# Prologue of a fused attention layer: GpSimd presets split in two, cond's silu and turn later, the embedding in another bank and reader step, five warm-up matmuls left out

## The reference: what is computed

```python
xn = layer_norm(x, norm_w, norm_b)                      # x: 8 x 512 x 256
q, k = xn @ q_w + q_b, xn @ k_w + k_b                   # 16 heads of 16
att = einsum('bnhl,bmhl->bnmh', q, k) + (1 - mask) * -1e6
att = softmax(att, axis=2)
v = (xn @ v_w + v_b) * src_mask
y = einsum('bnmh,bmhl->bnhl', att, v)
e = silu(emb) @ emb_w + emb_b                           # emb (cond): 8 x 512
scale, shift = split(e, 2)
h = layer_norm(y, sb_norm_w, sb_norm_b) * (1 + scale) + shift
out = x + silu(h) @ out_w + out_b
```

## Time and profile before

| | |
|---|---|
| time, median of 3 | 563.47 us |
| the profiled execution: its own time / its span | 564.25 / 562.5 us |
| TensorE matmul busy (PE) | 524.0 us, 93% |
| VectorE busy (DVE) | 416.9 us, 74% |
| ScalarE busy (ACT) | 371.4 us, 66% |
| GpSimd busy (POOL) | 194.2 us, 35% |
| mean granted TensorE clock | 0.997 |

### The profile page before, as it was taken

The page is one execution under the profiler, slowest core; times in us unless marked ns, Lnnn a source line. Parts: engine busy times, 40 slices in busy tenths (PEclk is TensorE's granted clock), DMA queues, the critical chain, the costliest instruction groups (busy, mean ns, idle before and its releaser), DMA issues.

```text
span 562.5 us, 10004 instructions
## 1 busy us (share of the span) xinstructions
PE 524.0 (93%) x2845; PEld 194.7 (35%) x2848; DVE 416.9 (74%) x661; ACT 371.4 (66%) x674; POOL 194.2 (35%) x237
## 2 busy tenths in 40 slices
PE   7888999999999999999999999999999999988886
PEld 3452223233343334333343233433342333422243
DVE  7588667787788778787787777877687867878425
ACT  2205776677757877577766877577766877667851
POOL 7244112443342512334333422425233422224003
PEclk9899999999999999999999999999999999999999
DMA  5632332433324332433424333333325323241021
GB/s 135 215 116 86 105 121 79 120 97 108 113 61 152 105 121 78 130 114 98 113 74 150 98 117 88 105 124 103 111 82 155 93 79 95 88 132 47 1 76 38
DMA packets 55050, 57.95 MB, mean 103 GB/s; under 512 B 12376, under 2 KB 42200, under 8 KB 55024
## 3 DMA queue, kind: packets, MB, share of 16 engines
q1 hardware_dynamic: 54480, 56.84, 34.0%
q10 hardware_dynamic: 544, 0.79, 0.5%
HBM read 36.35 MB, written 21.00 MB: 102 GB/s over the span
## 4 chain that ended last, share of the span: by engine, by line
PE 74%; DVE 11%; issue 7%; ACT 5%; DMA 1%; POOL 0%; ACTq 0%; POOLq 0%; DVEq 0%; SPq 0%
PE pv_ps L492 22%; PE st_ps L476 16%; PE mx_ps L450 11%; PE job_ps L533 9%; DVE negmax L776 8%; ACT probs L608 5%; PE job_ps L540 5%; PE job_ps L563 4%; PE mx_ps L460 1%; PE pv_ps L397 1%; PE job_ps L551 1%; DMA x_in<-in_x 1%; PE mx_ps L533 1%; PE mx_ps L540 0%; PE job_ps L424 0%
## 5 line engine op out<-in xcount | busy, mean ns | idle before, releaser
L776 DVE TENSOR_REDUCE negmax<-mx_ps 128x2 f32<-128x1024 f32 x256 | 301.4, 1220 | 106.9 <-PE mx_ps L450 106.3
L608 ACT ACTIVATE probs<-st_ps 128x512 f32<-128x512 f32 x512 | 277.9, 597 | 101.2 <-PE st_ps L476 98.2
L476 PE MATMUL st_ps<-q_rows,k_rows 115*128 115x512 bf16 x512 | 166.5, 384 | 14.1 <-ACT probs L608 6.0
L492 PE MATMUL pv_ps<-probs,v_rows 128*32 128x512 f32 x1024 | 136.4, 605 | 0.5 <-ACT probs L608 0.5
L1024 POOL TENSOR_TENSOR qk_rest<-qk_full,qk_parts 128x512 f32<-128x512 f32 x31 | 35.9, 1157 | 202.5 <-ACT qk_parts L620 202.5
L476 PEld LDWEIGHTS st_ps<-q_rows,k_rows 115*128 115x128 bf16 x512 | 39.5, 97 | 127.6 <-ACT probs L608 84.4
L450 PE MATMUL mx_ps<-k_rows,q_rows 51*128 51x512 bf16 x512 | 80.0, 381 | 2.0 <-DVE negmax L776 1.1
L533 PE MATMUL job_ps<-x_norm_t,w_qk 128*128 128x512 f32 x116 | 54.7, 593 | 0.6 <-DVE mod_half L763 0.6
L450 PEld LDWEIGHTS mx_ps<-k_rows,q_rows 51*128 51x128 bf16 x512 | 16.5, 94 | 109.4 <-issue 65.5
L1033 POOL TENSOR_TENSOR qk_parts<-qk_rest,qk_parts 128x512 bf16<-128x512 f32 x31 | 35.9, 1158 | 46.8 <-DVE qk_parts L851 38.9
L631 ACT ACTIVATE qk_full<-job_ps,qkb_col 128x512 f32<-128x512 f32 x29 | 19.9, 687 | 25.9 <-PE job_ps L533 25.9
(11 more groups left out here) (112 smaller groups left out, 400.1 us busy)
## 6 DMA issues: line engine op xcount, KB each, us to landing
qk_dram<-qk_parts SPq DMA_DIRECT2D x128, 128.0 KB
q_rows<-qk_dram SPq DMA_DIRECT2D x124, 96.0 KB
k_rows<-qk_dram SPq DMA_DIRECT2D x124, 96.0 KB
x_in<-in_x SPq DMA_DIRECT2D x16, 256.0 KB, 2.9
x_res<-in_x SPq DMA_DIRECT2D x8, 512.0 KB, 4.0
out<-out_sb SPq DMA_DIRECT2D x16, 256.0 KB, 2.6
w_e<-in_L_cond_emb_w SPq DMA_DIRECT2D x1, 1024.0 KB, 5.9
k_rows<-mask_dram SPq DMA_DIRECT2D x64, 6.0 KB
```

The lines of the kernel that those rows point to most:

```text
L476: pe.matmul(st_ps[u % ST_BANKS][:, :], k_rows[0:ROWS_ALL, g, h, c * P:(c + 1) * P], q_rows[0:ROWS_ALL, g, h, :], start=True, stop=True).th ...
L492: mm = pe.matmul(pv_ps[VW * h:VW * (h + 1), :], v_rows[:, c, g * GH + h, :], probs[:, t % P_SLOTS, h, :], start=(c == 0), stop=(c == CH - ...
L608: act.activation(probs[:, t % P_SLOTS, h, :], st_ps[u % ST_BANKS][:, :], ACT.Exp).then_inc(exp_done, 1)
L776: dve.tensor_reduce(by_pair[:, :, j, c], mx_ps[j][:, :, :], AXIS_X, ALU.max, negate=True).then_inc(max_done, 1)
```

## The change

Six things are edited, all in what body(-1) and step 0 of batch 0 issue:

1. GpSimd's presets of `q_rows` are made per half of the groups. `preset_q(0)` (three memsets for groups 0 and 1) runs at the start; `preset_q(2)`, and the presets of `v_rows` behind it, now wait for `part2_ready`, that is for VectorE's part 2 of group 0. They waited for `x_norm_ready`.
2. On VectorE `silu_of_cond` stands behind `first_parts`, and the copy of `mask_col` is the end of `mask_rows`.
3. `turn_cond` on TensorE moves from step 4 to step 8, behind proj 2; VectorE's copy of `cond_t` moves from the end of step 4 to the end of step 7.
4. The products of `embedding(m)` go to `pv_ps` instead of `job_ps`. Their wait for `v_plain_ready` is gone. The wait for `setup_done` moves from proj 3 in step 0 to the first `pv_step` of batch 0.
5. VectorE's `embedding()` stands behind the two reductions of step 0 instead of ahead of them.
6. The warm-up matmuls of steps 10 to 14 go to `st_ps[1]`, and the five of step 15 are left out.

```diff
-TURN_STEP = 4
+TURN_STEP = 8
@@ TensorE
-                    pe.wait_ge(v_plain_ready, 2)
-                    mm = pe.matmul(job_ps[:, m * B:(m + 1) * B], ...
+                    mm = pe.matmul(pv_ps[:, m * B:(m + 1) * B], ...
@@ max_quad, first group of batch 0
+                        pe.wait_ge(cond_ready, 1)
@@ pv_step
+                    if isinstance(b, int) and b == 0 and g == 0:
+                        pe.wait_ge(setup_done, 1)
@@ job
-                if isinstance(b, int) and b == 0 and t == 0:
-                    pe.wait_ge(setup_done, 1)
@@ body
-                    if isinstance(b, int) and b == -1 and t + MAX_LEAD >= STEPS:
-                        keep_warm(pv_ps, WARM_MAX)
+                    if isinstance(b, int) and b == -1 and STEPS - MAX_LEAD <= t < STEPS - 1:
+                        keep_warm(st_ps[1], WARM_MAX)
@@ VectorE, body(-1)
                     mask_rows()
+                    first_parts()
                     silu_of_cond()
-                    first_parts()
@@ VectorE, step
-                    if t == 0 and isinstance(b, int) and b == 0:
-                        embedding()
                     ...
                     stats_at(b, t, 2)
-                    if t == TURN_STEP and isinstance(b, int) and b == -1:
+                    if t == 0 and isinstance(b, int) and b == 0:
+                        embedding()
+                    if t == TURN_STEP - 1 and isinstance(b, int) and b == -1:
@@ GpSimd
-            pool.memset(q_rows[0:HALF + P // 4, :, :, :].bitcast(F32), 0.0).then_inc(q_preset, 1)
-            pool.wait_ge(q_preset, 1)
+            def preset_q(first):
+                groups, done = slice(first, first + 2), 3 * first // 2
+                pool.memset(q_rows[0:HALF + P // 4, groups, :, :].bitcast(F32), 0.0).then_inc(q_preset, 1)
+                ...
+            preset_q(0)
             def presets():
-                pool.wait_ge(x_norm_ready, CH)
-                pool.memset(q_rows[0:P // 4, :, 0:PAIRS, :].bitcast(F32), TWO_ONES).then_inc(q_preset, 1)
-                ...
+                pool.wait_ge(part2_ready, 1)
+                preset_q(NG // 2)
                 pool.memset(v_rows[:, :, :, :], 0.0).then_inc(pool_chain, 1)
@@ SyncE, rows of group 2 of batch 0
+                        sp.wait_ge(q_preset, 6)
```

More of the change, by code:

```diff
@@ L420, in embedding @@
                     pe.wait_ge(emb_loaded, EMB_DMAS * 16)
-                    pe.wait_ge(v_plain_ready, 2)
                 for k in range(KE):
-                    mm = pe.matmul(job_ps[:, m * B:(m + 1) * B], w_e[:, k, m * P:(m + 1) * P], cond_t[:, k, :],
+                    mm = pe.matmul(pv_ps[:, m * B:(m + 1) * B], w_e[:, k, m * P:(m + 1) * P], cond_t[:, k, :],
                                    start=(k == 0), stop=(k == KE - 1))
@@ L728, in mask_rows @@
                 dve.tensor_copy(mask_parts[:, 2, :], mask_rest[:, 1, :]).then_inc(maskp_ready, 1)
+                dve.wait_ge(mask_turned, 1)
+                dve.tensor_copy(mask_col[:, :, :], st_ps[0][:, 0:CH * B].rearrange("p (c b) -> p c b", b=B)
+                                ).then_inc(mask_col_ready, 1)
             def silu_of_cond():
@@ L736, in silu_of_cond @@
                 dve.tensor_scalar(cond_silu[:, :], cond_tanh[:, :], 0.5, None, ALU.mult).then_inc(silu_ready, 1)
-                dve.wait_ge(mask_turned, 1)
-                dve.tensor_copy(mask_col[:, :, :], st_ps[0][:, 0:CH * B].rearrange("p (c b) -> p c b", b=B)
-                                ).then_inc(mask_col_ready, 1)
             def first_parts():
@@ L753, in embedding @@
                 for m in range(2 * KD):
-                    dve.tensor_scalar(emb_t[:, m, :], job_ps[:, m * B:(m + 1) * B], eb_col[:, m:m + 1],
+                    dve.tensor_scalar(emb_t[:, m, :], pv_ps[:, m * B:(m + 1) * B], eb_col[:, m:m + 1],
                                       1.0 if m < KD else 0.0, ALU.add, ALU.add).then_inc(setup_chain, 1)
@@ L980, in _ @@
             pool.wait_ge(consts_ready, 1)
-            pool.memset(q_rows[0:HALF + P // 4, :, :, :].bitcast(F32), 0.0).then_inc(q_preset, 1)
-            pool.wait_ge(q_preset, 1)
-            def presets():
-                pool.wait_ge(x_norm_ready, CH)
-                pool.memset(q_rows[0:P // 4, :, 0:PAIRS, :].bitcast(F32), TWO_ONES).then_inc(q_preset, 1)
-                pool.wait_ge(q_preset, 2)
-                pool.memset(q_rows[HALF:HALF + P // 4, :, PAIRS:GH, :].bitcast(F32), TWO_ONES).then_inc(q_preset, 1)
-                pool.wait_ge(q_preset, 3)
+            def preset_q(first):
+                groups, done = slice(first, first + 2), 3 * first // 2
+                pool.memset(q_rows[0:HALF + P // 4, groups, :, :].bitcast(F32), 0.0).then_inc(q_preset, 1)
+                pool.wait_ge(q_preset, done + 1)
+                pool.memset(q_rows[0:P // 4, groups, 0:PAIRS, :].bitcast(F32), TWO_ONES).then_inc(q_preset, 1)
+                pool.wait_ge(q_preset, done + 2)
+                pool.memset(q_rows[HALF:HALF + P // 4, groups, PAIRS:GH, :].bitcast(F32), TWO_ONES).then_inc(q_preset, 1)
+                pool.wait_ge(q_preset, done + 3)
+            preset_q(0)
+            def presets():
+                pool.wait_ge(part2_ready, 1)
+                preset_q(NG // 2)
                 pool.memset(v_rows[:, :, :, :], 0.0).then_inc(pool_chain, 1)
```

## The result

The changed kernel takes 567.11 us, the median of 5 executions (565.17 to 567.31), against 563.53 us for the kernel before (563.24 to 563.88): ratio 1.0051, 95% interval 1.0033 to 1.0070. Measured again on another chip, the pair gave 566.18 against 563.89 us, ratio 1.0039 (1.0023 to 1.0055). The forecast was 563.4 us with a range up to 565.0. It is wrong: the kernel is slower, and outside the range.

The account below looks back on a forecast made before the run. The bound was taken to be group 0's copies and reads behind a full DMA queue, ahead of the first quad. Terms -0.67 + 0.6 + 0.0 = -0.1 gave 564.2 us for the profiled execution, 563.4 as median; range 561.7 to 565.0.

Parts of the forecast that it names:

- The second chain and the queue: Ahead of the first quad: group 0's copies wait behind loads in a full DMA queue, landing at 21.3 us.
- rival A: Group 0's copies follow part 2, landing 1.6 us earlier; first quad at 25.6, 561.6 us in all; chance 0.17.
- Presets and silu (edits 1, 2): Start of body(-1): mask casts 0.43 us each, mask split 3.2 us earlier, part 2 at 16.7; worth nothing.
- Turn in step 8 (edit 3): Ahead of the first quad: ScalarE's reads start with SyncE's, 0.67 us earlier; first quad at 27.2; -0.67 us.
- TensorE's clock at the first quad: A 4.3 us idle gap ahead of the first quad brings half clock onto the quads: +0.6 us, bounds 0 and 1.9.
- The light stretch at step 0: At 42.2 to 45.4 us without warm-ups; a clock fall there was only a rival, +1.9 us, chance 0.13.
- rival B: Clock falls once more at step 0, proj 3 and what follows at half rate: 565.3 us; chance 0.13.
- The moved wait (edits 4 and 5): Step 0: the wait moves from proj 3 to the first `pv_step` at the same price; 0.0, bounds -0.6 and +0.3.

Follow-up runs that it names:

- p1: Kernel before with edit 1 alone (presets split, half of them behind part 2 of group 0): 565.38 us, ratio 1.0028.
- q4: Changed kernel, step 15's warm-ups back, 22 warm-ups in step 8, batch 1's x and output weights loaded behind group 0's copies, embedding's bank released early: 562.90 us, ratio 0.9975.
- e4_bank: Changed kernel with step 15's warm-ups back, 26 warm-ups in step 8, and the embedding's bank released early to the first product with the values: 563.42 us, ratio 0.9990.
- fourth extra profile: Kernel before, unchanged, the last of four single profiled executions; full clock from 5.3 us on, first quad at 27.15: 563.68 us.
- after: The changed kernel with all six edits, against the kernel before, first measurement and its profile: 567.11 us, ratio 1.0051; profiled execution 565.17 us.
- e1: Changed kernel with the five warm-up matmuls of step 15 put back (also e1_warm15): 565.27 us, ratio 1.0019.
- again: Changed kernel measured once more on another chip, no edit: 566.18 us, ratio 1.0039.
- p3: Kernel before with edit 3 alone (transpose of cond's silu in step 8): 565.22 us, ratio 1.0019.
- e2_gap: Changed kernel with 26 warm-ups instead of 10 in step 8, filling the gap ahead of the first quad: 565.06 us, ratio 1.0011.
- e3_both: Changed kernel with 26 warm-ups instead of 10 in step 8 and the five of step 15 put back: 563.92 us, ratio 0.9992.
- the queue's first try: Changed kernel, step 15's warm-ups back, 18 in step 8, six loads behind group 0's reads: 572.01 us; with early bank release too, 571.52 us.

## Why the prediction was wrong, step by step

*The second chain and the queue: right for this change, and half of the story.* The copies of group 0 wait behind 2 MB of loads. Part 2 came 1.7 us earlier in p1 (16.65) and the reads did not; moving 0.8 MB of loads behind the copies moved the reads by 0.9 to 1.5 us. What the prediction held against rival A, "a full queue and not a late part 2", is not all: with late saves (q4 against e4_bank) the queue alone moves the reads by 0.07 us. The 2.8 us from the last save to the first read, which it gave as the argument for A, is a bound of its own and lay at the same place.

*Presets and silu (edits 1, 2), "worth: nothing": right in its times, wrong in what it left out.* The casts came to 0.02 us, the splitting of the mask to 0.3 us, part 2 in p1 to 0.1 us; in the changed kernel's profile part 2 is 1.0 us late with the clock. But edit 1 alone costs 1.6 us (565.38 against 563.74), since it too lets TensorE run ahead into a gap.

*Turn in step 8 (edit 3), -0.67: failed.* The mechanism is there (ScalarE's reads start with SyncE's, first quad 27.2), but the kernel before has it too where no low stretch delays ScalarE: its fourth extra profile shows it, and by the clock 69 of 103 executions are of that kind. The term was read from a profile whose ScalarE was late because of a low stretch at 18.2 to 21.6. The hint was on the table: the profiled execution took 564.25 us and the median was 563.47. I carried that difference over as a constant ("the median of the runs is 0.8 lower"), when it was the very loss that I was counting as a gain. 26 of 103 executions have 3.4 us at half clock, and take 564.25.

*TensorE's clock at the first quad, +0.6: the term that was mis-sized.* The gap was forecast (4.3 us; 3.2 to 4.2 in the profiles) and so was the fall. It measured +1.35 us (both versions on one chip), or +1.2 for edit 3 alone, over the 1.1 that the forecast's own range allowed and inside the bound of 1.9 that was named. I had priced a stretch of 1.7 to 4.7 us; in 10 of 12 executions with step 15's warm-ups the time at half clock is about twice the 3.4 us of the earlier trace rows. The trace of before showed one length, and I took it for the usual one. The rule of the Trainium skill quoted there (TensorE: Matmul & The Clock Gate), that such a wait for a DMA makes the next work start cold, holds in three profiles with the gap (after, e1, p1): the clock falls ahead of the first quad, which takes 1.03 us in place of 0.6. In two (again, p3), behind waits of 4.20 and 4.10 us, the quad still runs at full clock and the fall comes 0.6 to 1.2 us behind its start. That the place varies from run to run is so.

*The light stretch at step 0: the second step that failed, rival B at 0.13.* I worked out its place, 42.2 to 45.4, its price, 1.9, and gave it little since the clock there was 1.00 before. But before, five warm-ups filled it; that row was no evidence about the stretch without them. It happens in at least 8 of 12 executions of the changed kernel: seven have 10 us or more at half clock, which none of e1_warm15 has, and the profiled one has it with 6.8 in all. With the warm-ups alone left out, 7 of 12 have 6 us or more, against 8 of 103 with them. Over all executions the price is 1.14 us (0.85 by means); in e2_gap the executions with 3.4 us at half clock lie some 1.5 us above those with none. "In place of 1.05 us of warm-ups TensorE waits" was right for its time and left out what the warm-ups were for.

*The moved wait (edits 4 and 5), 0.0: right in the wait*, 0.60 us for 0.64. From the first quad to the first product with the values there are 20.45 us in the full-clock profiles of e2_gap and e3_both, against 20.69 in those of the kernel before, so the part as a whole may be worth -0.2, inside its bounds; no run takes it by itself.

The sum as it should have stood: 563.7 at full clock, 0 for the turn, +1.35 and +1.14 for the two falls, 566.2. The second measurement gave 566.18; the first gave 567.11, for three of its five executions are of the upper group.

## What to carry to other kernels

Taking a wait away from an engine doesn't take it out of the program: it moves to the next thing that the engine waits for, and on TensorE it may there cost clock as well. Ask of every gap that a change opens what runs behind it, and of every warm-up that it removes which stretch it was filling. Before reading a term out of a profile, compare the profiled execution's time with the median: if it is longer, find what was special in it, for the change may "gain" only that. And a transfer's landing is bound by what stands ahead of it in the queue or by its own issue, whichever is later, so a test of one shows nothing while the other ends at the same place; when something is moved behind it, the next group's transfers are what it stands ahead of.

## What the runs showed of the hardware that I had not expected

- The first rise of the clock came at 3.9 to 10.7 us in the profiles of kernels that start alike. Where it came by 5.5, proj 0 mostly started at 11.4 to 11.7; in the four profiles where it came at 9.1 to 10.7, at 12.6 to 13.1. The two profiles of the queue's first try, with 12.0 and 12.6 at an early rise, show that something else can move it too. Without the pause of some 1 us at 5 us the rise came at 7.2 in the one profile, and six executions lay within 0.24 us.
- Low stretches came in lengths of 3.4 us and of 6.8 us (one of 23.9 in the run whose embedding waited for its load). Two of 6.8 (26.1 to 33.0, 45.3 to 52.2) had TensorE busy for 2.37 and 2.77 us of their first 3.4, and all the time in the rest.
- In the kernel before the four copies, 0.52 MB, took about 3 us (an estimate from the rates of the earlier trace rows) at a DMA share of 0.45 to 0.55, where the loads ahead of them ran at 0.95 and more. Why the share is half is not shown.
